# Routed down products with the weights loaded, and their results scattered from PSUM by VectorE and ScalarE

## The chip, the cores and the metric

The kernel runs on one core of a Trainium2 chip. The metric is the device time of one execution in microseconds. Engines: PE (TensorE) multiplies matrices into PSUM; DVE (VectorE), ACT (ScalarE) and POOL (GpSimd) work on elements; SP's queue issues DMAs. Each engine runs its instructions in the order of its program, and they wait for each other through semaphores.

## The reference

Input x has 128 rows (batch) of 32 positions of 128 channels. A first block adds a quantized linear layer on a layer norm to x. What the change touches is the mixture of experts behind it: each of the 128 rows picks two of eight experts, all its 32 positions go through both, and a shared expert runs over all rows.

```python
w, sel = jax.lax.top_k(rw, TOP_K)
w = w / w.sum(axis=-1, keepdims=True)
...
dense_w = jnp.zeros((B, E), x.dtype).at[jnp.arange(B)[:, None], sel].add(w)

def step(acc, params):
    g, u, d, we = params
    return (acc + we[:, None, None] * _gemma_mlp(x, g, u, d), None)
out, _ = jax.lax.scan(step, jnp.zeros_like(x), (skill_gate, skill_up, skill_down, dense_w.T))
out = out + _gemma_mlp(x, shared_gate, shared_up, shared_down)
```

`_gemma_mlp` is gelu(x gate) * (x up), times down, with an inner width of 512. Its sum goes into a last quantized block with 384 inner channels, whose first step needs the largest magnitude of the whole sum.

## The kernel before

**Numbers.** A product of fp32 precision is made of three fast ones: each operand is split in a high part and the rest (`Hh` and `Hl` for the hidden values, plane 0 and 1 of `WD` for the down weights), and high*high, high*low and low*high are added in PSUM.

**Stages.** First (0 to 64 us in the profile) the layer norm, in twelve steps `n`, with the routing worked out beside it on DVE: `S[:, 42]` and `S[:, 43]` become the slots of each row's two choices, `S[:, 38]` and `S[:, 39]` their weights, `ordI` the row of each slot, `etI` the expert of each tile. Then the quantized layer and the first eight steps of the shared expert (`J0` = 2 blocks of four), up to 96 us. Then the routed tiles.

**Routed tiles.** The (row, expert) pairs are sorted by expert into tiles of `SL` = 8 slots; `NM` = 36 tiles are always run. A slot has 32 positions, so a tile is 256 columns. For tile `i`, POOL's `fetch(i)` copies the eight rows' columns from `XT` to `xg`, with the address of each row in a register that is loaded from `ordI`. SP loads the tile's gate and up weights into `Wr`. PE's `unit(i, u)` makes gate and up products into the PSUM banks `BG[u]` and `BU[u]` for u = 0, 1. ACT's `gelu_of` writes `Gb`, DVE's `hidden_of` multiplies with `BU[u]` into `HbS`, ACT's `high_of` makes `Hh`, DVE's `low_of` makes `Hl`. PE's `down(i)` stands after the units of tile `i+1`. The hidden values are loaded as weights and the down weights stream past (256 columns with `Hh`, 128 with `Hl`), at an address in `WD` from a register (`expert_of`). The result has the positions on the partitions. DVE's `sum_y` adds its two halves into `Yb`, and SP's `store_y` writes it to DRAM.

**Rest of the shared expert.** Steps `n` = 8 to 33: PE makes `shared_up(n)` and `shared_down(n-2)`, ACT and DVE the same operations as above on 512 columns. The low part is made by POOL for m < 4 and 16 to 29, else by DVE (`on_pool`). POOL gathers each row's two results from DRAM into `G0` and `G1` by an indirect DMA; ACT scales one, DVE adds the other (`WEIGHS`), PE transposes four blocks of 128 (`TURNS`), and the result is added into `C`. `LARGEST` says at which step the largest magnitude of a block is taken.

**The first turn of a maximum.** At the end of the layer norm DVE reduces eight columns to one (`d_col`), PE transposes it (`turn_max`), DVE reduces again (`top`), and PE spreads the value. PE runs products without use (`busy`) in between. The scale of the quantized layer hangs on this.

Of the kernel before, what the change touches and what calls it, by code (L numbers as in the profile page):

```python
# [14 lines left out]
X = mybir.AxisListType.X  # L15
ADD, SUB, MUL = ALU.add, ALU.subtract, ALU.mult
# [7 lines left out]
XR = 4  # L24
RM = 12582912.0
J0 = 2
EARLY = J0 + 3
# [14 lines left out]
def program(nc, x, cond, Wb, bb, As, Bs, fw, gamma, beta, sg, su, sd, hg, hu, hd, wg, wu, wd, out):  # L42
    ctx = ExitStack()
    with ctx:
# [14 lines left out]
        def sem(name):  # L59
# [6 lines left out]
        X1 = at("X1", [128, T, 128], F32)  # L66
        identF = at("identF", [128, 128], F32)
# [11 lines left out]
        C = at("C", [128, T, 128], F32)  # L79
# [7 lines left out]
        Yb = at("Yb", [128, 4, 2, 128], F32)  # L87
        off[0] = RQ + 24576
        tern = at("tern", [128, 128], BF16)
        SHh = [at(f"SHh{m}", [128, 512], F32R) for m in range(2)]  # L90
# [5 lines left out]
        C_i = at("C_i", [128, 4096], I16)  # L96
# [21 lines left out]
        ioi = at("ioi", [128, NSLOT], I32)  # L118
        bcI = at("bcI", [128, 1], I32)
# [21 lines left out]
        G0 = at("G0", [128, T, 128], F32, R1)  # L141
        G1 = at("G1", [128, T, 128], F32, R1 + 16384)
# [10 lines left out]
        assert RH == R1 + 106496  # L153

        wscr = nc.dram_tensor("wscr", (E * 128, 2048), F32, kind="Internal").ap()
        yscr = nc.dram_tensor("yscr", (SL * NT, 4096), F32, kind="Internal").ap()
# [9 lines left out]
        s_fill = sem("s_fill")  # L166
        s_yw = [sem(f"s_yw{i}") for i in range(4)]
        s_yz = [sem(f"s_yz{i}") for i in range(NT - NM)]
        s_got = [sem(f"s_got{i}") for i in range(4)]
        s_ob = sem("s_ob")  # L170
# [9 lines left out]
        d_rt, d_w2, d_hot, d_absw, d_place, d_parts, d_tern, d_ord, d_et, d_slot = (  # L180
            sem(n) for n in ("d_rt", "d_w2", "d_hot", "d_absw", "d_place", "d_parts", "d_tern", "d_ord", "d_et", "d_slot"))
# [8 lines left out]
        a_wdh, k_wdl = sem("a_wdh"), sem("k_wdl")  # L190
# [4 lines left out]
        k_xg, p_eg, p_eu, a_eg, d_eh, a_ehh, d_ehl, p_ed, d_ey = (  # L195
            sem(n) for n in ("k_xg", "p_eg", "p_eu", "a_eg", "d_eh", "a_ehh", "d_ehl", "p_ed", "d_ey"))
        d_bits, d_k, a_k0, p_kt, a_kc, p_wf, a_wf, d_wf, d_mxc = (
# [30 lines left out]
        def on_pool(m):  # L228
            return m < 4 or 16 <= m <= 29
# [8 lines left out]
        def flat(A, j):  # L238
            return A[:, 4 * j:4 * j + 4, :].rearrange("p t c -> p (t c)")
# [68 lines left out]
        def _(e):  # L308
# [127 lines left out]
            def shared_up(n):  # L436
# [4 lines left out]
                if n >= 2:  # L441
                    w.wait_ge(a_sg, n - 1)
# [1178 lines left out]
```

## Time and profile before

| | us |
|---|---|
| median of 3 runs | 443.53 |
| lowest, highest | 442.97, 444.92 |
| profiled execution | 443.94 |
| its span | 441.9 |
| PE busy | 381.9 (86%) |
| DVE busy | 324.9 (74%) |
| ACT busy | 267.2 (60%) |
| POOL busy | 247.3 (56%) |
| PE's share of the chain that ended last | 64% |

The page splits the span in 40 slices and gives the busy share of each engine in tenths; PE has a 9 in nearly all slices from 110 to 320 us, which are the routed tiles and the shared blocks behind them. Busy shares are means over stages that have different limits, so stretches have to be read one by one. A queue's own instructions (register work, waits) don't count as busy; a view by line names them as POOLq, DVEq or ACTq.

### The profile page before, as it was taken

Reading aid. Unit: us, or ns where it says so; the run is one execution under the profiler, and the core shown is the slowest. Engines: PE = TensorE matmul, PEld = TensorE weight load, DVE = VectorE, ACT = ScalarE, POOL = GpSimd, SP = SyncE. Lnnn points to the kernel's source line nnn. Section 1 sums busy time; section 2 is a strip of 40 time slices with the busy share of each in tenths; the row PEclk is TensorE's granted clock in tenths of the full one; section 3 lists DMA queues with packets and bytes.
Section 4 is the critical chain, followed back from the end, with each engine's and each line's share of the span. In section 5 each row is a group of like instructions: output and inputs, shape, how many; then the busy total and the mean of one; then the engine's idle time right before and its main releaser. Section 6 shows DMA issues by size and latency. Waiting matters only on the chain.

```text
span 441.9 us, 8331 instructions
## 1 busy us (share of the span) xinstructions
PE 381.9 (86%) x2497; PEld 333.0 (75%) x2497; DVE 324.9 (74%) x562; ACT 267.2 (60%) x397; POOL 247.3 (56%) x429
## 2 busy tenths in 40 slices
PE   5888987987999999999999999999999985002997
PEld 4566765667999999999999999877767753001797
DVE  3585647845688877776776776644976989989894
ACT  3556578853545544544544544677647789999660
POOL 1465744856677765665665500744528357895252
PEclk9996999998999999999999999999999999555899
DMA  8799852065677777677677631640000000000022
GB/s 265 281 317 346 306 169 85 1 216 197 233 247 259 248 252 275 233 253 269 229 257 269 229 114 40 227 155 0 0 1 0 0 2 0 1 0 0 1 95 97
DMA packets 30440, 68.14 MB, mean 154 GB/s; under 512 B 3487, under 2 KB 18850, under 8 KB 25762
## 3 DMA queue, kind: packets, MB, share of 16 engines
q1 hardware_dynamic: 27770, 63.19, 41.1%
q0 software_dynamic: 1152, 4.19, 2.7%
q8 instruction: 22, 0.36, 0.3%
q10 hardware_dynamic: 1472, 0.20, 0.3%
q14 instruction: 24, 0.20, 0.1%
HBM read 51.98 MB, written 15.60 MB: 153 GB/s over the span
## 4 chain that ended last, share of the span: by engine, by line
PE 64%; DVE 13%; ACT 8%; POOL 6%; issue 5%; DMA 3%; POOLq 0%; SPq 0%; DVEq 0%; ACTq 0%
PE ps L315 61%; DVE S L671 6%; PE ps L312 3%; DVE O_i L668 1%; ACT xnT L1146 1%; POOL Hl L1367 1%; DMA wscr<-wst 1%; DMA Wr<-wscr 1%; DVE G L662 1%; ACT ps L1146 1%; ACT U L1146 1%; DMA S<-in_cond_dram 1%; DVE S L662 1%; POOL t_i L1364 1%; POOL WD L1367 1%
## 5 line engine op out<-in xcount | busy, mean ns | idle before, releaser
L1424 POOL CAST xg<-XT 128x64 fp32r x288 | 102.3, 404 | 57.8 <-PE ps L315 48.7
L1146 ACT ACTIVATE Gb<-ps 128x512 f32<-128x512 f32 x104 | 62.2, 598 | 92.2 <-PE ps L315 92.0
L315 PE MATMUL ps<-xg,Wr 128*128 128x256 f32 x864 | 112.5, 287 | 3.6 <-issue 2.7
L662 DVE TENSOR_TENSOR HbS<-Gb,ps 128x512 f32<-128x512 f32 x104 | 71.3, 687 | 57.9 <-PE ps L315 56.0
L315 PEld LDWEIGHTS ps<-xg,Wr 128*128 128x128 f32 x864 | 106.9, 193 | 4.2 <-issue 2.9
L1146 ACT ACTIVATE Hh<-HbS 128x512 fp32r<-128x512 f32 x104 | 65.1, 627 | 12.8 <-DVE HbS L662 12.5
L315 PE MATMUL ps<-WD,Hh 128*128 x288 | 68.6, 328 | 0.0
L662 DVE TENSOR_TENSOR Hl<-HbS,Hh 128x512 fp32r<-128x512 f32 x86 | 63.7, 758 | 1.3
L315 PE MATMUL ps<-WD,Hl 128*128 x288 | 64.1, 223 | 0.0
L315 PEld LDWEIGHTS ps<-WD,Hl 128*128 128x128 f32 x288 | 55.2, 192 | 0.0
L315 PEld LDWEIGHTS ps<-WD,Hh 128*128 128x128 f32 x288 | 54.5, 189 | 0.0
L315 PE MATMUL ps<-XT,SHh 128*128 128x512 f32 x144 | 50.9, 405 | 0.0
L1146 ACT ACTIVATE ps<-G,S 128x1024 int32<-128x1024 f32 (+1 forms) x29 | 35.6, 1249 | 6.7 <-DVE O_i L668 6.2
L1367 POOL TENSOR_TENSOR Hl<-HbS,Hh 128x512 fp32r<-128x512 f32 x18 | 23.2, 1291 | 18.1 <-ACT Hh L1146 18.1
L315 PEld LDWEIGHTS ps<-XT,SHh 128*128 128x128 f32 x144 | 27.0, 188 | 5.1
L671 DVE TENSOR_REDUCE S<-G 128x1 f32<-128x1024 f32 (+1 forms) x25 | 28.0, 1165 | 0.6 <-ACT G L1146 0.5
L671 DVE TENSOR_REDUCE Yb<-ps 128x128 f32<-128x256 f32 x72 | 26.7, 410 | 0.6 <-PE ps L315 0.6
L1367 POOL TENSOR_TENSOR wst<-stg,wst 128x512 fp32r<-128x512 f32 x16 | 20.5, 1303 | 9.0 <-ACT wst L1146 9.0
L315 PE MATMUL ps<-XT,SHl 128*128 128x512 f32 x64 | 25.0, 390 | 0.0
L1452 POOL DMA_INDIRECT G<-yscr,sidx x8 | 8.2, 1020 | 28.3 <-issue 28.3
L315 PE MATMUL ps<-Hh,SD 128*128 128x512 f32 x64 | 21.2, 412 | 2.1 <-DVE Hl L662 1.4
L1364 POOL TENSOR_SCALAR G<-O_i 128x1536 f32<-128x1536 int16 (+2 forms) x12 | 12.6, 1047 | 18.0 <-DVE O_i L668 17.9
(191 smaller groups left out, 693.3 us busy)
## 6 DMA issues: line engine op xcount, KB each, us to landing
Wr<-wscr SPq DMA_DIRECT2D x36, 1024.0 KB, 5.0
wscr<-wst SPq DMA_DIRECT2D x16, 512.0 KB, 4.8
yscr<-Yb SPq DMA_DIRECT2D x36, 128.0 KB, 2.7
stg<-n_L_cond_skill_gate_dram SPq DMA_DIRECT2D x8, 256.0 KB, 6.4
stg<-in_L_cond_skill_up_dram SPq DMA_DIRECT2D x8, 256.0 KB, 6.4
wdr<-n_L_cond_skill_down_dram SPq DMA_DIRECT2D x8, 256.0 KB, 4.1
out_dram<-X SPq DMA_DIRECT2D x7, 256.0 KB, 2.0
X<-in_x_dram SPq DMA_DIRECT2D x3, 512.0 KB, 6.8
```

Of the source, the lines that this page charges most:

```text
L312: return e.transpose(o_, i_, identF[:, :])
L315: return e.matmul(o_, l, r, start=start, stop=stop, skip_group_check=True)
L662: return e.tensor_tensor(o_, a, b, op)
L668: return e.scalar_tensor_tensor(out=o_, in0=a, scalar=s, in1=b, op0=op0, op1=op1)
L671: return e.tensor_reduce(o_, i_, X, op, apply_absolute_value=absv)
L1146: return e.activation(o_, i_, func, **kw)
L1364: return e.tensor_scalar(o_, a, s1, s2, op0, op1)
L1367: return e.tensor_tensor(o_, a, hi.bitcast(F32), SUB)
L1424: last = e.tensor_copy(xg[:, i % XR, :, T * s:T * s + T].rearrange("p a t -> p a t"), XT[:, :, :, bass.ds(regs[s], 1)].rearrange("p a t o ...
L1452: e.indirect_dma_start(out=D[:, 8 * p:8 * p + 8, :].rearrange("p t c -> p (t c)"), out_offset=None, in_=yscr.rearrange("n (q c) -> (n q) c ...
```

## The change

The down product of a tile is turned round: the tile's down weights are loaded as PE's weights and the hidden values stream past in 256 columns, so the result has the channels on its partitions and the positions in its columns, as the shared expert's has. PE takes the weights from a fixed place: POOL copies the tile's 1024 columns out of `WD` into one of two buffers `WT` (`down_weights`), which lie where X1 begins. X1 is therefore written to DRAM (`xscr`) before and read back after the last routed tile.

The result stays on the chip. `DD` holds, for each choice, 128 channels by 32 positions by 136 columns, of which 128 are rows. For each slot an operation reads 32 columns of PSUM, multiplies with the slot's weight (`Wt`) and writes them into its row's column of each position, at an address from a register that is loaded from `colI`. Tiles of even number are scattered by DVE, odd ones by ACT. Two new tables are made beside the layer norm: `colI`, the column of each slot, and `Wt`, its weight on all partitions, both by sums over the partitions on PE.

Behind the routed tiles POOL adds the two choices (`PAIRED`), DVE the shared expert's result; the gather, the scaling, the transposes and `C` are gone. POOL makes all low parts of steps 8 to 29. The core of the diff:

```diff
-                for h in range(2):
-                    Z = BY[b][:, 256 * h:256 * h + 256]
-                    both = Z.rearrange("p (a n) -> p a n", a=2)
-                    for q in range(4):
-                        w.wait_ge(d_ehl, 2 * i + 1 + q // 2)
-                        mm(both, Hh[:, 2 * b + q // 2, half(q, h)], WD[:, :, bass.ds(expert[i] + 128 * q, 128)], q == 0, False)
-                        last = mm(Z[:, 0:128], Hl[:, 2 * b + q // 2, half(q, h)], WD[:, 0, bass.ds(expert[i] + 128 * q, 128)], False, q == 3)
+                w.wait_ge(k_wt, i + 1)
+                Z = BY[b][:, 0:256]
+                for q in range(4):
+                    w.wait_ge(a_ehh, 2 * i + 1 + q // 2)
+                    xh, xl = (A[:, 2 * b + q // 2, 256 * (q % 2):256 * (q % 2) + 256] for A in (Hh, Hl))
+                    wh, wl = (WT[:, i % 2, a, 128 * q:128 * q + 128] for a in range(2))
+                    mm(Z, wh, xh, q == 0, False)
+                    mm(Z, wl, xh, False, False)
+                    w.wait_ge(d_ehl, 2 * i + 1 + q // 2)
+                    last = mm(Z, wh, xl, False, q == 3)
...
-            def sum_y(i):
+            def scatter(i):
+
+                w.wait_ge(d_tab, 8)
+                at_ = nc.values_load_multi_w_load_instructions(
+                    colI[0:1, SL * i:SL * i + SL], engines=(mybir.EngineType.DVE,), skip_runtime_bounds_check_because=WHY)[1]
                 w.wait_ge(p_ed, i + 1)
...
+                for s in range(SL):
+                    last = ts(spot(at_[s]), BY[pair(i)][:, T * s:T * s + T], Wt[:, SL * i + s:SL * i + s + 1], None, MUL)
                 last.then_inc(d_ey, 1)
...
+                        if u == 0 and i >= 2 and i % 2:
+                            scatter(i - 2)
...
+            def down_weights(i):
+
+                at_ = nc.values_load_multi_w_load_instructions(
+                    etI[0:1, 0, i:i + 1], engines=(mybir.EngineType.Pool,), skip_runtime_bounds_check_because=WHY)[1][0]
...
+                e.tensor_copy(WT[:, i % 2, :, :], WD[:, :, bass.ds(at_, 512)]).then_inc(k_wt, 1)
...
-            busy(12, bank[2], WbTh[:, :], xTh[:, 0, :])
+            w.wait_ge(d_tab, 6)
+            mm(bank[4][0:1, 0:NSLOT], ones[:, 0:1], tmpP[:, :], True, False)
+            mm(bank[4][0:1, 0:NSLOT], ones[:, 0:1], tmpQ[:, :], False, True).then_inc(p_tab, 1)
+            mm(bank[3][:, 0:NSLOT], ones[:, :], Pm[:, :], True, False)
+            mm(bank[3][:, 0:NSLOT], ones[:, :], iof[:, :], False, True).then_inc(p_tab, 1)
+            busy(7, bank[2], WbTh[:, :], xTh[:, 0, :])
...
+                if m in PAIRED:
+                    j = PAIRED[m]
+                    w.wait_ge(*spread_of(NM - 2))
+                    w.wait_ge(*spread_of(NM - 1))
+                    e.tensor_tensor(choice(0, j), choice(0, j), choice(1, j), ADD).then_inc(k_dd, 1)
```

How the instructions stand is shown at three places. PE, one down product of the routed stage, before (WD down weights, Hh and Hl hidden values, ISA a register instruction; the pair of products comes eight times, the first four times with ISA ahead):

```order
L315 ISA [waits d_ehl,d_ey]
L315 MATMUL ps<-WD,Hh 128x256
L315 MATMUL ps<-WD,Hl 128x128
L315 ISA
L315 MATMUL ps<-WD,Hh 128x256
L315 MATMUL ps<-WD,Hl 128x128
L315 ISA [waits d_ehl]
```

and now, all of it (WT the copied down weights):

```order
L341 MATMUL ps<-Hh,WT 128x256 [waits a_ehh,k_wt,d_ey]
L341 MATMUL ps<-Hh,WT 128x256
L341 MATMUL ps<-Hl,WT 128x256 [waits d_ehl]
L341 MATMUL ps<-Hh,WT 128x256 x2
L341 MATMUL ps<-Hl,WT 128x256
L341 MATMUL ps<-Hh,WT 128x256 [waits a_ehh]
L341 MATMUL ps<-Hh,WT 128x256
L341 MATMUL ps<-Hl,WT 128x256 [waits d_ehl]
L341 MATMUL ps<-Hh,WT 128x256 x2
L341 MATMUL ps<-Hl,WT 128x256
```

Sixteen products with register addresses became twelve without, and they wait for POOL's copy (k_wt).

DVE, one tile of the same stage before (Yb the summed down result):

```order
L671 TENSOR_REDUCE Yb<-ps 128x128 [waits p_ed,s_yw1]
L671 TENSOR_REDUCE Yb<-ps 128x128
L662 TENSOR_TENSOR HbS<-Gb,ps 128x512 [waits a_eg,d_ehl,p_eu] x2
L662 TENSOR_TENSOR Hl<-HbS,Hh 128x512 [waits a_ehh] x2
L662 TENSOR_TENSOR WQ<-WQ,S 128x1152 [waits d_bits]
```

and now the end of an odd tile and the start of an even one (colI the table of columns, DD the scattered result; the last two rows come six times more, then HbS follows):

```order
L672 TENSOR_TENSOR HbS<-Gb,ps 128x512 [waits a_eg,d_ehl,p_eu] x2
L672 TENSOR_TENSOR Hl<-HbS,Hh 128x512 [waits a_ehh] x2
L675 TENSOR_SCALAR S_54<-S_54 128x36 [waits d_bits]
L962 TENSOR_LOAD colI
L675 ISA [waits p_ed]
L675 ISA x2
L675 TENSOR_SCALAR DD<-ps,Wt 128x32
L675 ISA x3
L675 TENSOR_SCALAR DD<-ps,Wt 128x32
```

Two reductions per tile became, every second tile, one load of registers, 24 register instructions and eight small operations, and they stand ahead of the tile's HbS.

ACT, two tiles of the same stage before (Gb the Gelus, Hh the high parts):

```order
L1146 ACTIVATE Gb<-ps 128x512 [waits p_eg] x2
L1146 ACTIVATE Hh<-HbS 128x512 [waits d_eh,p_ed]
L1146 ACTIVATE Hh<-HbS 128x512 [waits d_eh]
L1146 ACTIVATE Gb<-ps 128x512 [waits p_eg] x2
L1146 ACTIVATE Hh<-HbS 128x512 [waits d_eh,p_ed]
```

and now the end of an even tile and the start of an odd one, again with six more of the last two rows, then the second Gb:

```order
L1169 ACTIVATE Hh<-HbS 128x512 [waits d_eh,p_ed]
L1169 ACTIVATE Hh<-HbS 128x512 [waits d_eh]
L1169 ACTIVATE Gb<-ps 128x512 [waits p_eg]
L1274 TENSOR_LOAD colI
L1169 ISA [waits p_ed]
L1169 ISA x2
L1169 ACTIVATE DD<-ps,Wt 128x32
L1169 ISA x3
L1169 ACTIVATE DD<-ps,Wt 128x32
```

The same instructions as DVE's now stand between the two Gelus of every second tile.

## Rows read from the trace of the kernel before

**Rows 1.** Stretches, us: busy (instructions) of PE, PEld, DVE, ACT, POOL; clock; DMA; GB/s.

```profile
110.00:268.00 158.00, 158.00 (x1342) 158.00 (x1340) 120.48 (x207) 79.31 (x135) 90.94 (x249) 1.00 0.68 237
268.00:328.00 60.00, 58.62 (x283) 46.80 (x282) 40.77 (x65) 38.01 (x68) 26.23 (x22) 1.00 0.22 76
```

**Rows 2.** Timeline, a tile: start, length, engine, line, operation, out<-in, idle before.

```profile
188.18 3.08 PE L315 MATMUL ps<-xg,Wr 128*128 128x256 f32 x24
189.15 0.60 ACT L1146 ACTIVATE Gb<-ps 128x512 f32<-128x512 f32 x1 [1.21 <-PE ps L315]
189.88 0.69 DVE L662 TENSOR_TENSOR HbS<-Gb,ps 128x512 f32<-128x512 f32 x1 [0.48 <-PE ps L315]
...
191.07 0.62 ACT L1146 ACTIVATE Hh<-HbS 128x512 fp32r<-128x512 f32 x1
191.10 0.28 PE L315 MATMUL ps<-WD,Hh 128*128 x1
...
191.91 1.53 DVE L662 TENSOR_TENSOR Hl<-HbS,Hh 128x512 fp32r<-128x512 f32 x2
...
192.90 3.08 PE L315 MATMUL ps<-xg,Wr 128*128 128x256 f32 x24
193.37 0.74 DVE L671 TENSOR_REDUCE Yb<-ps 128x128 f32<-128x256 f32 x2
```

**Rows 3.** Timeline of POOL, three fetches that follow each other.

```profile
111.06 2.95 POOL L1424 CAST xg<-XT 128x64 fp32r x8 [0.93 <-PE ps L315]
114.39 1.97 POOL L1424 CAST xg<-XT 128x64 fp32r x8 [0.38 <-PE ps L315]
117.72 2.01 POOL L1424 CAST xg<-XT 128x64 fp32r x8 [1.36 <-issue]
```

**Rows 4.** Lines L1416, L916, L1238, their queue instructions: ns shortest/median/longest.

```profile
L1416 POOLq FUSED_REGOPS  x288: 147/147/185, 90.3 to 246.6; - x144
L1416 POOLq TENSOR_LOAD <-ordI x36: 561/565/1718, 89.5 to 244.4; - x36
...
L916 DVEq FUSED_REGOPS  x1: 222/222/222, 93.7 to 93.7; - x1
...
L1238 ACTq FUSED_REGOPS  x1: 167/167/167, 95.5 to 95.5; - x1
```

**Rows 5.** Groups by shape: busy us, mean ns of one, idle time before.

```profile
L665 DVE TENSOR_SCALAR ST<-ps 128x4 f32<-128x4 f32 x8 | 1.2, 154 | 3.9 <-PE ps L315 3.8
L668 DVE SCALAR_TENSOR_TENSOR Pm<-iof,S,tmpP 128x312 f32<-128x312 f32 x1 | 0.6, 610 | 0.0
L665 DVE TENSOR_SCALAR tmpP<-iof,S 128x312 f32<-128x312 f32 x1 | 0.4, 366 | 0.0
...
L315 PE MATMUL ps<-hs,BT 128*128 128x512 f32 x16 | 8.3, 603 | 0.0
...
L1424 POOL CAST xg<-XT 128x64 fp32r x288 | 102.3, 404 | 57.8 <-PE ps L315 48.7 <-issue 9.1
L1367 POOL TENSOR_TENSOR Hl<-HbS,Hh 128x512 fp32r<-128x512 f32 x18 | 23.2, 1291 | 18.1 <-ACT Hh L1146 18.1
L1364 POOL TENSOR_SCALAR U_i<-U,S 128x1024 int16<-128x1024 f32 x12 | 13.3, 1127 | 0.6 <-DVE S L1112 0.3 <-POOL t_i L1364 0.2
```

**Rows 6.** Timeline, the last maximum of the layer norm and its first turn.

```profile
62.45 0.69 DVE L671 TENSOR_REDUCE S<-xnT 128x1 f32<-128x512 f32 x1 [0.79 <-ACT xnT L1146]
...
63.39 0.27 PE L312 MATMUL ps<-identF,S 128*1 128x128 f32 x1 [0.29 <-DVE S L671]
...
64.34 1.88 PE L315 MATMUL ps<-xTh,WbTh 128*128 128x512 f32 x7
```

**Rows 7.** Chain that ended last: start, us, what.

```profile
277.71 2.08 PE ps L315 x9
...
292.90 0.45 PE ps L312 x4
...
297.98 0.45 PE ps L312 x4
```

More of the change, by code:

```diff
@@ L24 @@
 XR = 4
+DW = 136
 RM = 12582912.0
 J0 = 2
-EARLY = J0 + 3
 class Waits:
@@ L165, in program @@
         s_wz = [sem(f"s_wz{i}") for i in range(NT - NM)]
[L166 to L170, printed above, removed]
+        s_xs = [sem(f"s_xs{i}") for i in range(2)]
+        s_xr, s_ob = sem("s_xr"), sem("s_ob")
         k_const, d_const = sem("k_const"), sem("d_const")
@@ L217, in program @@
         NG, NR, HK = 2 * E, 2 * E + 3, 4 * J0
-        IOTA, PART, TRI0, IDENT, TRI, CTR, HALVES, MEAN = 3, 4, 5, 6, 7, 8, 9, 10
+        IOTA, PART, TRI0, IDENT, TRI, CTR, HALVES, MEAN, PLACES = 3, 4, 5, 6, 7, 8, 9, 10, 11
         SPLITS = (0, 2, 2, 3, 3, 2, 2, 2, 0, 3, 0, 0)
-        WEIGHS = {16: 5, 18: 6, 20: 7, 22: 0, 24: 1, 25: 2, 27: 3, 28: 4}
-        TURNS = {n + 2: j for n, j in WEIGHS.items()}
-        LARGEST = {25: (0,), 26: (5,), 27: (1,), 28: (2,), 30: (3,), 32: (6, 4), 33: (7,)}
-        WEIGHED = list(WEIGHS.values())
-        ENDED = [0, 5, 1, 2, 6, 3, 4, 7]
+        ENDED = [2, 0, 3, 1, 4, 5, 6, 7]
+        PAIRED = {9: 2, 11: 0, 13: 3, 15: 1, 17: 4, 19: 5, 21: 6, 23: 7}
+        ADDED = list(PAIRED.values())
+        LARGEST = {14: 2, 16: 0, 18: 3, 20: 1, 22: 4, 26: 5, 30: 6, 33: 7}
+        WHY = "made from the slots' rows alone"
         def on_pool(m):
-            return m < 4 or 16 <= m <= 29
+            return m < 4 or HK <= m <= 29
         def low_at(m):
@@ L827, in _ @@
                     w.wait_ge(d_rt, n_)
-                    for p in range(4):
-                        ts(sidx[:, 2 * p:2 * p + 2], S[:, 42:44], 4.0, float(p), MUL, ADD).then_inc(d_slot, 1)
                 if n == 5:
@@ L984, in _ @@
                         low_of(i, u)
-                    w.wait_ge(s_yw[i % 4], 16 * (i // 4))
-                    sum_y(i)
-                for r in range(NT - NM):
-                    w.wait_ge(s_yz[r], 16)
+                    if i % 2 == 0:
+                        scatter(i)
             w.passed = passed
@@ L1246, in high_of, with scatter @@
                 do(Hh[:, 2 * pair(i) + u, :], HbS[:, u, :]).then_inc(a_ehh, 1)
+            def scatter(i):
+                w.wait_ge(d_tab, 8)
+                at_ = nc.values_load_multi_w_load_instructions(
+                    colI[0:1, SL * i:SL * i + SL], engines=(mybir.EngineType.Activation,), skip_runtime_bounds_check_because=WHY)[1]
+                w.wait_ge(p_ed, i + 1)
+                for s in range(SL):
+                    last = do(spot(at_[s]), BY[pair(i)][:, T * s:T * s + T], ACT.Identity, scale=Wt[:, SL * i + s:SL * i + s + 1])
+                last.then_inc(a_ey, 1)
             for i in range(NM + 1):
@@ L1264, in _ @@
                     shared_high(HK)
+            scatter(NM - 1)
             passed = dict(w.passed)
@@ L1274, in _ @@
                         high_of(i, u)
-                w.wait_ge(d_ey, NT)
-                for r in range(NT - NM):
-                    w.wait_ge(s_yz[r], 16)
+                    if i % 2:
+                        scatter(i)
             w.passed = passed
```

235 lines of the change are left out of this document (114 added, 121 removed).

## The prediction, made before the changed kernel ran

> **What bounds the kernel now.** I read the table of stretches first. From 110 to 268 us, the stage of the routed tiles, PE is busy for all 158.00 us, at full granted clock, while DVE is busy for 120.48, ACT for 79.31 and POOL for 90.94 [rows 1]. So in this stage PE sets the pace, and the other engines wait for it. The timeline of one tile shows the pace: the gate and up products of one tile start at 188.18 and those of the next at 192.90, so a tile takes 4.72 us. Its 24 gate and up products fill 188.18 to 191.10, 0.122 us each; its 16 down products fill the other 1.80 us, 0.1125 each, although half of them have only 128 columns [rows 2]. In the same rows one sees the chain that runs beside PE: the first Gelu on ACT 0.60 us, the product Gb*up on DVE 0.69, the high part on ACT 0.62, two low parts on DVE 1.53 together, two sums of the down result 0.74. DVE has 1.38 + 1.53 + 0.74 = 3.65 us of work per tile and ACT 1.20 + 1.25 = 2.45, so both have over a microsecond to spare. The next stage, 268 to 328, is also PE's (58.62 of 60.00 busy) [rows 1].
>
> **What it means to address by a register.** This change lives on it, so I price it before anything else. POOL already does it in the kernel before: one fetch is 33 instructions that are not waits (a TENSOR_LOAD of eight numbers, 16 register instructions, then eight times one register instruction and a copy). Where POOL isn't held by others, fetches start at 111.06, 114.39 and 117.72, which is 3.33 us apart, although the eight copies take only 1.97 to 2.95 us of that [rows 3]. The difference is the register work: at POOL's queue a TENSOR_LOAD takes 565 ns and each of the eight larger register instructions 147 ns [rows 4]. So a slot costs (3.33 - 0.565) / 8 = 0.35 us in the queue of POOL, far more than its arithmetic.
>
> The changed kernel's scatter of one tile has again 33 such instructions: one TENSOR_LOAD, and eight times three register instructions and one small operation. The small operation itself is short: a DVE operation of 128x4 out of PSUM took 154 ns [rows 5], eight would be 1.2 us. The queue is what costs. The same larger register instruction, seen once each, took 222 ns on DVE and 167 ns on ACT against 147 on POOL [rows 4]. Scaled by that, a slot is 0.35 x 222/147 = 0.52 us on DVE and 0.39 on ACT; unscaled it is 0.35 on both. I take the middle of each, 0.43 on DVE and 0.37 on ACT, since the two scaled values rest on one instance each; the ends stay in the range. A scatter is then 8 x 0.43 = 3.44 us on DVE and 8 x 0.37 = 2.96 on ACT, with a TENSOR_LOAD of 0.57 ahead of each. These eight groups stand behind the wait for the down product, so they can't be done early by the program's order.
>
> The Trainium skill (Advanced Engine Details and Errata, Clock Domains) has VectorE's sequencer at 0.96 GHz where the others run at 1.2, a factor of 1.25; by that a DVE slot would be 0.44 us. The rows agree in direction (222 against 147) and go further.
>
> **Part 1, the down products.** Now 12 products of 256 columns per tile in place of 16 (the change's section shows the order). At 0.122 us each that is 1.46 us in place of 1.80, and PE's tile falls from 4.72 to 36 x 0.122 = 4.39 us: -0.33 us per tile, if PE stays what sets the pace. PE also loses its own register work, which was hidden already since PE was never idle [rows 1].
>
> **Part 2, the scatters, which I expect to set the pace.** Even tiles go to DVE, ahead of the two products Gb*up of the tile two later; odd ones to ACT, between its two Gelus. Both engines run their queues in order, so each scatter holds up everything behind it, and the chain passes from one to the other. Over two tiles, from one DVE scatter to the next: the scatter 3.44; both Gb*up of the even tile 2 x 0.69 = 1.38; hand-over to ACT 0.13 (a Gelu ends at 189.75, DVE starts at 189.88 [rows 2]; I use this for all four); the high part and the Gelu of the odd tile are only passed on to ACT's data path, then its TENSOR_LOAD 0.57; the ACT scatter 2.96; the second Gelu 0.60; hand-over 0.13; Gb*up 0.69; 0.13; high part 0.63; 0.13; the low part is only passed on, then DVE's TENSOR_LOAD 0.57, and the next scatter follows. Sum 11.36 us for two tiles. PE needs 2 x 4.39 = 8.78 for them and the kernel before takes 9.44. So this closed chain is the longest, and the tile takes 5.68 us. PE then waits at the up products, because the bank of the last one is freed by the Gb*up that stands behind the scatter. There are 17 such pairs: 17 x (11.36 - 9.44) = **+33 us**. With 0.35 for every slot the pair is 10.5 us and the term +18; with 0.52 and 0.39, and 0.3 more for DVE's TENSOR_LOAD, 12.5 us and +52.
>
> What goes with the scatters: the sums (0.74 us of DVE per tile [rows 2]), the stores of the tiles, the gather; none of them held PE, so they give nothing back. SP loses the stores and gets eight writes of X1 before the first tile and eight reads after the last, both far from any wait that ends late.
>
> **Part 3, POOL.** Behind each fetch stands a copy of the tile's down weights, 128x1024. Its queue costs 0.57 + 0.35 = 0.92 us; with the fetch 4.25 us per tile, under 5.68, and the copy itself (a POOL operation of that size took 1.13 us [rows 5]) runs beside the next register work. The weights of a tile are copied two tiles ahead. I cost this at nothing; if its cover is gone it is a rival below.
>
> **Part 4, the tables, before 64 us.** DVE gets six operations of 128x312 in the last steps of the layer norm. One of them took 0.61 and a simpler one 0.37 us [rows 5]. Two (0.98) stand straight ahead of the last product xnT, one (0.37) between the last maximum and the overall one; the rest falls into DVE's idle time. So the last maximum, at 62.45 in [rows 6], ends near 64.1 and the last table operation near 64.5. PE waits for that operation, then makes four products of 312 columns in full fp32 and seven fillers, and only then turns the maximum. A full fp32 product of 512 columns is two of the 16 instructions that took 8.3 us [rows 5], so 1.04 us, and 0.63 for 312 columns: 2.5 us; seven fillers took 1.88 [rows 6]. The turn comes at 64.5 + 2.5 + 1.9 = 68.9 in place of 63.39: +5.5. All that follows hangs on this scale. Two more DVE operations in the quantization add about 0.3. **+5.8 us**, 4 to 7.
>
> **Part 5, the rest of the shared blocks, 268 to 328.** Eight groups of four transposes leave, 0.45 us each: -3.6. In three places PE waited for POOL's low part behind ACT's extra copies (the chain has 5.08 us from the transposes at 292.90 to those at 297.98, for two steps of 2.08 and four transposes of 0.45, 4.6 us; so again twice after that [rows 7]): -1.4. But POOL now makes all the low parts (1.29 us each [rows 5]) and eight adds of the same size between them. A step is 2.08 us, and two low parts and one add take 3.9 of 4.16; the low part behind an add comes about 0.5 us late, and PE has nearly no slack for it: +4. At the start the last ACT scatter stands ahead of a Gelu: +1.5. Sum +0.5, from -4 to +3.
>
> **The sum.** The profiled execution took 443.94 us (span 441.9). 443.9 + 33 + 5.8 + 0.5 = 483.2. The median of the runs is 0.4 lower: **483 us**.
>
> **Rivals.**
> Faster: the register work runs beside the data paths and the scatters cost only their small operations. Then PE sets the pace, a pair takes 8.78, 17 x -0.66 = -11; with parts 4 and 5 it is 439 us. For it: PE's register work was hidden entirely. The Trainium skill (Advanced Engine Details and Errata, Sequencer and Instruction Queues) says too that other engine instructions can be queued while a control instruction is executed; the trace agrees only in that copies of 1.97 and of 2.95 us give the same 3.33. Against it: POOL's fetches are 3.33 us apart with 1.97 of copies [rows 3]. It decides at the price of a slot: the pair without slots is 4.96 us, so the change as a whole loses nothing once a pair is at most 9.44 - 6.3/17 = 9.07, which is 0.26 us per slot. Chance 0.14.
> Each engine alone: the slots cost what I say, but the scatters overlap in time rather than follow each other. DVE's queue is 2 x (1.38 + 1.53) + 3.44 = 9.2 us per pair: 443.9 - 4 + 6.3 = 446. Against it: the second Gb*up needs the Gelu behind ACT's scatter. Chance 0.09.
> POOL: copy, register work and fetch add up instead of overlapping, 3.33 + 0.92 + 1.13 = 5.4 us per tile, and copies on POOL stretch: their mean is 404 ns [rows 5], while undisturbed they follow each other by 0.25 [rows 3]. With 0.9 more, 6.3 us: 470 to 500 us. The Trainium skill (SBUF — State Buffer) says that a VectorE instruction with two SBUF inputs contends with a GpSimd one that reads SBUF, which DVE's low parts are; the 404 ns agree with it. Chance 0.08.
>
> **How the numbers follow.** The forecast, 462 to 507 by its bounds (443.9 + 18 + 4 - 4, and + 52 + 7 + 3), has 0.69, POOL's case 0.08, the single engines 0.09, the faster one 0.14. A measurement of this kernel can tell about 0.5%, 2.2 us, from no change. Faster 0.14; within it 0.05, from the 446 case; slower 0.81. The range goes from 446 to 505 and leaves out the faster case and the top of the forecast.
>
> **What would show it.** In the profile after: PE busy for some 75 to 80% of the routed stage, waiting for DVE's Gb*up at the up products; two tiles in 11.4 us; DVE's and ACT's small operations at 0.35 to 0.52 us from one to the next although each takes under 0.25; POOL with idle time; the first turn of a maximum near 69 us. I am wrong if the small operations follow each other at under 0.26 us, if PE stays without a gap, or if DVE's and ACT's scatters lie in the same time.

## The result, and the profile after

The changed kernel took 476.4 us (median of 4 runs, 475.0 to 479.1) beside 444.2 us for the kernel before (4 runs): 1.074 times the time before, with a 95% interval of 1.067 to 1.080. The prediction was 483 us, slower. The profiled execution took 479.12 us (span 477.3), the slowest of the four; before it was 443.94 (span 441.9).

First the table of stretches of the changed kernel, with the columns of [rows 1]:

```profile
66.00:73.00 7.00, 7.00 (x17) 3.81 (x16) 0.00 (x0) 0.24 (x2) 0.00 (x0) 0.56 0.34 138
116.00:300.00 184.00, 158.18 (x1216) 154.94 (x1216) 132.52 (x278) 111.57 (x265) 126.91 (x293) 0.95 0.53 187
```

In the routed stage PE is busy for 86% of the time where it was busy for all of it [rows 1], and its granted clock is 0.95. (The prediction's sign was 75 to 80%; products at the lower clock take longer and count as busy all the while.) The new first row is a stretch in which PE works at 0.56 of its clock and DVE and ACT do nothing; I come back to it. Who waits for whom is in the table of waits (us in total, times, longest):

```profile
ACT Hh L1169 <- DVE HbS L672: 70.4, 39, 4.2
POOL WT L1467 <- PE ps L341: 46.3, 26, 5.0
DVE HbS L672 <- ACT Gb L1169: 37.4, 21, 3.6
...
PE ps L341 <- DVE HbS L672: 26.8, 17, 2.5
```

ACT waits for DVE, DVE waits for ACT, and PE waits 17 times for DVE's `HbS`: once in each pair of tiles but the first, and once behind the last, in the shared blocks. POOL waits for PE. That is a closed chain of two engines with PE behind it. One pair, in the timeline:

```profile
184.78 2.85 DVE L675 TENSOR_SCALAR DD<-ps,Wt 128x32 f32 x8
...
187.52 1.27 DVE L672 TENSOR_TENSOR HbS<-Gb,ps 128x512 f32<-128x512 f32 x2
188.25 2.42 PE L341 MATMUL ps<-xg,Wr 128*128 128x256 f32 x18 [0.42 <-DVE HbS L672]
188.29 1.17 ACT L1169 ACTIVATE Hh<-HbS 128x512 fp32r<-128x512 f32 x2 [2.70 <-DVE HbS L672]
...
189.85 2.49 ACT L1169 ACTIVATE DD<-ps,Wt 128x32 f32 x8
...
192.92 0.69 DVE L672 TENSOR_TENSOR HbS<-Gb,ps 128x512 f32<-128x512 f32 x1 [1.97 <-ACT Gb L1169]
...
195.35 3.08 DVE L675 TENSOR_SCALAR DD<-ps,Wt 128x32 f32 x8 [0.31 <-issue]
```

It reads as the prediction's chain: DVE's scatter, the product Gb*up behind it, ACT's scatter between its two Gelus, the second Gelu, and DVE's product that waited 1.97 us for it. The chain of work that ended last goes through two of DVE's products in each pair, one behind DVE's scatter and one behind ACT's. Of those behind ACT's, the first, two in the middle and the last are

```profile
116.02 0.70 DVE HbS L672
...
182.13 0.70 DVE HbS L672
...
192.92 0.69 DVE HbS L672
...
302.75 0.70 DVE HbS L672
```

so 17 pairs take 302.75 - 116.02 = 186.7 us, **10.98 us a pair** (predicted 11.36; 9.44 before).

A mean hides that the pairs are of two kinds, long ones and short ones; that is taken up further on. The rest of the difference is found by landmarks that both programs have: the last square of the layer norm, the first turn of a maximum [rows 6], the first product of the first tile, the first product of the remaining shared blocks, the overall maximum, the end. Such a table takes out the start of the program, up to the last square, which took between 55.8 and 60.4 us in thirteen profiles whatever the kernel, and which hides differences of a few us in single executions.

| stretch, us | before | after | difference | predicted |
|---|---|---|---|---|
| start to last square | 56.07 | 56.20 | +0.1 | 0 |
| to the first turn | 7.32 | 16.63 | +9.3 | +5.5 |
| to the first tile | 32.53 | 35.67 | +3.1 | +0.3 |
| the routed tiles | 172.50 | 194.34 | +21.8 | +33 |
| remaining shared blocks, to the maximum | 60.58 | 62.13 | +1.6 | +0.5 |
| to the end | 112.90 | 112.33 | -0.6 | 0 |
| sum (span) | 441.9 | 477.3 | +35.4 | +39.3 |

The landmarks of after, from its timeline:

```profile
72.83 0.28 PE L338 MATMUL ps<-identF,S 128*1 128x128 f32 x1
...
108.50 7.48 PE L341 MATMUL ps<-xg,Wr 128*128 128x256 f32 x48 [2.02 <-DMA Wr<-wscr]
...
302.84 0.40 PE L341 MATMUL ps<-XT,SHh 128*128 128x512 f32 x1
```

### The profile page after: what moved, and what is told of

Its sections match the earlier page's. It is cut to its first block, busy times and chain, and to the rows that moved or that the text cites. A ratio compares the mean times of both kernels' runs of the same rounds, so it can differ in the third digit from the quotient of the medians.

```text
span 477.3 us, 8947 instructions
## 1 busy us (share of the span) xinstructions
PE 385.0 (81%) x2324; PEld 328.4 (69%) x2324; DVE 329.4 (69%) x622; ACT 295.7 (62%) x527; POOL 297.7 (62%) x474
## 4 chain that ended last, share of the span: by engine, by line
DVE 26%; PE 25%; ACT 19%; issue 12%; POOL 9%; DMA 4%; DVEq 3%; ACTq 2%; POOLq 0%; SPq 0%
PE ps L341 23%; ACT Hh L1169 6%; DVE DD L675 5%; DVE HbS L672 5%; ACT DD L1169 5%; DVE S L681 4%; DVE Hl L672 4%; DVEq L675 3%; ACT Gb L1169 3%; POOL Hl L1393 2%; ACTq L1169 2%; PE ps L338 2%; DMA wbr<-in_L_cond_W_base_dram 1%; DVE O_i L678 1%; DMA Wr<-wscr 1%
## 5 line engine op out<-in xcount | busy, mean ns | idle before, releaser
L341 PE MATMUL ps<-xg,Wr 128*128 128x256 f32 x864 | 122.0, 298 | 27.8 <-DVE HbS L672 25.8
L341 PEld LDWEIGHTS ps<-xg,Wr 128*128 128x128 f32 x864 | 115.2, 205 | 31.5 <-DVE HbS L672 29.1
L1467 POOL CAST WT<-WD 128x1024 fp32r x36 | 38.2, 1062 | 48.0 <-PE ps L341 46.3
L341 PE MATMUL ps<-Hh,WT 128*128 128x256 f32 x288 | 55.3, 290 | 0.0
L675 DVE TENSOR_SCALAR DD<-ps,Wt 128x32 f32 x144 | 38.4, 277 | 18.6 <-issue 5.5
L1393 POOL TENSOR_TENSOR Hl<-HbS,Hh 128x512 fp32r<-128x512 f32 x26 | 34.4, 1324 | 24.8 <-ACT Hh L1169 24.8
L341 PEld LDWEIGHTS ps<-Hh,WT 128*128 128x128 f32 x288 | 47.0, 200 | 0.1
L1169 ACT ACTIVATE DD<-ps,Wt 128x32 f32 x144 | 44.9, 321 | 1.9 <-issue 1.2
L341 PE MATMUL ps<-Hl,WT 128*128 128x256 f32 x144 | 41.5, 288 | 0.0
L1169 ACT ACTIVATE ps<-G,S 128x1024 int32<-128x1024 f32 (+1 forms) x29 | 35.6, 1249 | 6.0 <-DVE O_i L678 5.4
L341 PEld LDWEIGHTS ps<-Hl,WT 128*128 128x128 f32 x144 | 28.6, 198 | 0.0
L341 PE MATMUL ps<-XT,SHl 128*128 128x512 f32 x64 | 26.2, 409 | 0.0
```

The source lines that it names most:

```text
L341: return e.matmul(o_, l, r, start=start, stop=stop, skip_group_check=True)
L675: return e.tensor_scalar(o_, a, s1, s2, op0, op1)
L1169: return e.activation(o_, i_, func, **kw)
L1393: return e.tensor_tensor(o_, a, hi.bitcast(F32), SUB)
L1467: e.tensor_copy(WT[:, i % 2, :, :], WD[:, :, bass.ds(at_, 512)]).then_inc(k_wt, 1)
```

## The experiments

Two theories for the 21.8 us: the **closed chain** (two scatters that follow each other through DVE and ACT) against its rivals (POOL's queue, each engine's own queue, register work that costs nothing). And for the 12.4 us ahead of the first tile: the tables, in PE's part or in DVE's. All experiments start from the changed kernel, the last four with two repairs in it. They ran on two chips: known addresses, ACT's scatter at the end of the tile, more work for POOL and both parts of the tables moved on one, all others on the other. Ratios are to the kernel before on the same chip, which took 442.1 us on the first and 443.1 to 443.4 on the second.

### Addresses known in advance

```diff
-                at_ = nc.values_load_multi_w_load_instructions(
-                    colI[0:1, SL * i:SL * i + SL], ...)[1]
+                at_ = [(8 * (i // 2) + s) % 128 for s in range(SL)]
...
-                    last = ts(spot(at_[s]), BY[pair(i)]...
+                    last = ts(DD[:, at_[s]:at_[s] + DW * (T - 1) + 1:DW], BY[pair(i)]...
```

(ACT's likewise.) 

> The changed kernel with scatters that write to columns known in advance: the same eight small operations of 128x32 on DVE or ACT for each tile, at the same places of the queues, but no TENSOR_LOAD and no register instruction. It leaves out the placement by token; all else is computed. Theory that the register work in the queue sets the price: the small operations follow each other at 0.15 to 0.2 us, the scatter falls from 2.8 us on DVE and 2.5 on ACT to 1.2 to 1.6, the loads of 0.6 go, the closed chain of two tiles falls from the measured 10.98 us to about 8.2, below PE's 8.78, and PE sets the pace: 17 x -2.2 = -37, so 439 us. Rival, that the operation itself costs what its row says (277 ns on DVE, 321 on ACT): two tiles take about 10.1 and the time is 461. Rival, that POOL sets the pace: 470 or more.

Measured: 435.6 us (434.5 to 436.9), 0.984 of before (0.978 to 0.991). One scatter of each engine in its timeline:

```profile
197.59 1.38 DVE L675 TENSOR_SCALAR DD<-ps,Wt 128x32 f32<-128x32 f32 x8
...
201.26 1.57 ACT L1168 ACTIVATE DD<-ps,Wt 128x32 f32<-128x32 f32 x8
```

Eight operations take 1.38 and 1.57 us, 0.17 and 0.20 each, although a single one still shows 269 and 344 ns: they overlap. PE's groups of 24 products start at 191.21, 195.53 and 199.85, so a tile takes 4.32 us, PE's 36 products at 0.12. The routed stage takes 155.26 us. The stage of the changed kernel took 191.5 to 194.3 us in its profiles, so its scatters cost it 36 to 39 us by their register addressing. The rest of the change gives 17 us there against before (172.5 - 155.3): 36 tiles of 0.40 us less are 14.4 of them, the others lie in a hole of the kernel before that comes up below. The theory that the register work sets the price holds; both rivals (461 and 470 or more) fell, and the time is 3 us under the 439 that I expected.

### ACT's scatter at the end of the tile

```diff
                         gelu_of(u, 2 * i + u + 1)
-                        if u == 0 and i >= 2 and i % 2:
-                            scatter(i - 2)
...
                         high_of(i, u)
+                    if i >= 2 and i % 2:
+                        scatter(i - 2)
```

> The changed kernel with one call moved on ACT: the scatter of an odd tile stands behind the two high parts of the tile, at its end, no longer between its two Gelus. No instruction is added or removed. Theory of the closed chain: the second Gb*up no longer waits for ACT's scatter, DVE's and ACT's scatters lie in the same time, and DVE's own queue, 2 x (1.38 + 1.38) + 2.85 + 0.57 = 8.9 us, or PE with 8.78, sets the pace in place of 10.98 for two tiles: 17 x -1.9 to -2.2, so 439 to 444 us. Rival, that one engine's own queue sets the pace already (each engine alone, or POOL): nothing changes, 476.

Measured: 450.9 us (446.6 to 451.7), 1.020 (1.014 to 1.026). Not an instruction less, and the routed stage takes 165.4 us, 26 to 29 less than the changed kernel's 191.5 to 194.3. The timeline shows both scatters in the same time:

```profile
190.06 2.60 ACT L1169 ACTIVATE DD<-ps,Wt 128x32 f32 x8 [0.26 <-issue]
...
190.87 3.08 DVE L675 TENSOR_SCALAR DD<-ps,Wt 128x32 f32 x8 [0.19 <-issue]
...
193.84 1.28 DVE L672 TENSOR_TENSOR HbS<-Gb,ps 128x512 f32<-128x512 f32 x2
```

and the products behind DVE's scatter start at 184.69, 193.84 and 202.99: 9.15 us a pair, DVE's own queue (expected 8.9; the two low parts of a tile took 1.81 and 1.39 us in this pair where I had 1.38). The closed chain stands, and "the queue of one engine sets the pace" falls for the changed kernel: it became nearly true only here, where DVE still waits 0.16 us for ACT's high parts in each tile. The time misses my 439 to 444. The pair above was 0.25 us longer than my sum, and others are longer still: from 118.25 to 267.34 the 16 pairs take 8.8 to 10.4 us, 9.32 in the mean, which is 7 us in all. And I had started from 476.4, while the changed kernel took 480.4 when it ran again (below, on the other chip).

### ACT's scatter behind both Gelus, ahead of the high parts

```diff
-                        if u == 0 and i >= 2 and i % 2:
+                        if u == 1 and i >= 2 and i % 2:
```

> The changed kernel with ACT's scatter behind both Gelus of the odd tile but still ahead of its two high parts. Nothing is added or removed. Theory of the closed chain: the high parts now wait for the scatter, the low parts for them, and DVE's next scatter stands behind these: from one DVE scatter to the next 2.9 + 0.69, up and gate of the odd tile on PE 1.5, Gelu 0.6, ACT's load and scatter 0.5 + 2.4, two high parts 1.2, low part 0.8, about 10.5 us in place of 10.98, so 470 to 478 us. Rival, that only the second Gelu matters and everything behind it has slack: as with the scatter at the tile's end, 447 to 452.

Measured: 483.1 us (480.9 to 486.7), 1.087. The rival (447 to 452) fell, and the time is also above my 470 to 478. The chain was longer than my sum of 10.5: its pairs took 11.00 to 12.29 us, 11.36 in the mean from 133.55 to 303.97. Even the short ones are 0.5 above the sum, which I can't place. In the long ones PE's half clock is one of the reasons, since here a link of the chain runs through PE. In the pair from 191.01 to 202.50, 11.49 us, it was slow:

```profile
191.75 3.45 PE L341 MATMUL ps<-xg,Wr 128*128 128x256 f32 x18 [2.13 <-DVE HbS L672]
```

18 products in 3.45 us; in the changed kernel's pair above they took 2.42. So it is not enough to take the scatter from between the Gelus; it has to stand behind everything that DVE waits for.

### More work for POOL, and the changed kernel again

```diff
+                if i:
+                    w.wait_ge(k_wt, i)
+                for s in range(2 if i >= 2 else 0):
+                    e.tensor_copy(scr[:, 2, s, :], WDf[:, bass.ds(at_, 32)])
                 e.tensor_copy(WT[:, i % 2, :, :], WD[:, :, bass.ds(at_, 512)]).then_inc(k_wt, 1)
```

> The changed kernel with more work on POOL: ahead of each copy of down weights from the third tile on two more register-addressed copies of 128x32, about 0.35 us each in its queue, 0.7 us for each tile. Theory: POOL waits for PE for over a microsecond in each tile and has room for it: no change, 476 us, within 1.5 us. Rival, that POOL's queue is part of what sets the pace: 34 x 0.7 = 24 us more, 500.

> The changed kernel itself once more, as the measure for the runs beside it. The start of the program (the loads of the weights up to the last square of the layer norm) has taken between 56 and 60 us in the profiles so far, whatever the kernel; so single profiles are compared stretch by stretch from that square on, and times on the same chip. By the first runs 476.4 us beside 444.2; the kernel with more work on POOL took 479.1 beside 442.1. Theory that POOL has room: this run too comes to 477 to 480 beside it, and the routed stage takes the same 191.5 us. Rival, that POOL's extra work did cost: 473 to 475 here.

Measured: 479.1 us (477.0 to 480.8) with the extra copies, 480.4 (476.9 to 482.7) without. The groups of the first show that the work was done and where its time came from:

```profile
L1472 POOL COPY scr<-WD 128x32 f32 x68 | 14.1, 237 | 33.5 <-PE ps L343 27.5 <-issue 5.7
```

POOL still waited 27.5 us for PE ahead of them, and the routed stage took 191.5 us (193.0 without). POOL is no part of the chain. (The time is above my 476 by 3 us, and so is that of the changed kernel itself.) The two ran on different chips, so the stage and the ratios (1.085 and 1.080, intervals 1.078 to 1.092 and 1.071 to 1.088) say more than the times. 480.4 us is also the measure for the runs on the second chip, 4 us more than the first time; the first chip has none of its own.

### The tables moved

PE's part alone: the four products stand behind the first shared blocks, where PE waits for `Wr`, and the twelve fillers are back (DVE's two operations that read their results go with them).

```diff
             w.wait_ge(a_zg, 8)
-            w.wait_ge(d_tab, 6)
-            mm(bank[4][0:1, 0:NSLOT], ones[:, 0:1], tmpP[:, :], True, False)
...
-            busy(7, bank[2], WbTh[:, :], xTh[:, 0, :])
+            busy(12, bank[2], WbTh[:, :], xTh[:, 0, :])
             turn_max(0, bank[6], S[:, 180:181])
```

> The changed kernel with only PE's part of the tables moved: the four products stand behind the first shared blocks and the twelve fillers ahead of the first turn again, while DVE's six table operations stay where the change put them. From the last square to the first turn: 7.3 us before, 15.2 to 16.6 with the change, 8.0 to 8.4 with both parts moved. Theory: DVE's operations ahead of the last product xnT cost 2.3 us and the one ahead of the overall maximum 0.4, PE's wait, its products at half its clock and its fillers the rest; so 10.0 us from the last square to the turn, and 475 us beside the 480.4 of the changed kernel. Rival, that DVE's operations are most of it: 13 us or more, and 478.

With DVE's part too: `tmpQ` behind the last product `xnT`, `Pm` and `iof` behind the scale.

> The changed kernel with its tables moved: PE makes the four table products after the last product of the first shared blocks, ahead of the first tile, where it waits for Wr anyway; PE has its twelve fillers ahead of the first turn of a maximum again, and DVE makes the last three table operations behind the last product xnT and behind the scale, not ahead of them. The scatters are as they were. The changed kernel's first turn stood at 72.83 us, that of the kernel before at 63.39. My theory: those 9.4 us come back, less 0.3 to 1 for the operations in their new places, and of the 3.1 us that the stretch from the turn to the first tile got longer some 1 to 2, because PE's granted clock was lower there; from 476.4 to between 465 and 468 us, with the turn at 63.5 to 64.5. By the prediction's own size for this part it would be 5.8 us: 470.6. Rival: the late start is absorbed further on, since the first tile waits for its weights: 473 to 476.

Measured: 470.4 us (468.2 to 471.6) for PE's part alone, beside 480.4 for the changed kernel on that chip, and 472.0 us (469.4 to 472.3) for both on the other chip. Both times miss what I expected, 475 and 465 to 468. The two can't be told apart by their times, but can by the stretch from the last square to the turn, which came out at 9.78 us where I expected 10.0:

| us | before | change (6 profiles) | PE's part moved | both moved (5 profiles) |
|---|---|---|---|---|
| last square to first turn | 7.32 | 15.2 to 16.6 | 9.78 | 8.0 to 8.4 |
| turn to first tile | 32.53 | 33.7 to 35.7 | 33.58 | 33.4 to 34.4 |

So PE's part costs 5.4 to 6.8 us and DVE's operations 1.4 to 1.8. How PE's part came to that is in the changed kernel's timeline:

```profile
61.11 0.97 DVE L678 SCALAR_TENSOR_TENSOR tmpQ<-iof,S,tmpQ 128x312 f32<-128x312 f32 x1
62.01 1.38 DVE L675 TENSOR_SCALAR Pm<-iof,S 128x312 f32<-128x312 f32 x1
...
64.77 0.69 DVE L681 TENSOR_REDUCE S<-xnT 128x1 f32<-128x512 f32 x1 [0.79 <-ACT xnT L1169]
...
65.95 1.20 PE L341 MATMUL ps<-tmpP,ones 128*1 128x312 f32 x2 [5.46 <-DVE iof L675]
...
69.91 3.08 PE L341 MATMUL ps<-xTh,WbTh 128*128 128x512 f32 x7
```

PE waited 5.46 us for the last table operation, and then ran at the lower clock: its four products filled 65.95 to 69.9 (3.9 us; I had 2.5) and seven fillers took 3.08 us where seven of the same products took 1.88 before [rows 6]. The kernel before kept PE at work here; the change took five of the twelve fillers away and put a wait in their place.

### Both repairs, and what could be had beyond

> Both repairs together: ACT's scatter at the end of the odd tile and the tables behind the first shared blocks. If the two terms are independent, the stretch from the last square to the first turn takes 8.4 us (15.4 without it), the 36 tiles 9.15 us for two, and the time is 450.9 - 7 = 444 us, 441 to 446; that is the time of the kernel before. Rival, that the start is then held by the weights of the first tile: 448 to 451.

> The kernel with both repairs once more, as the measure for the run beside it and against the kernel before: 441 us beside 443 by the first time (0.995 of it). Theory: the two terms, 26 to 30 us from the scatters' chain and 7 to 8 from the tables, are all that the change lost; what is left is 2 us less than before, from PE's tile that fell from 4.72 to 4.58. So 0.993 to 0.997 of the kernel before.

Measured: 441.2 us (10 runs, 438.0 to 443.5), 0.995 of before (0.991 to 0.999), and 440.3 (12 runs), 0.996 (0.992 to 1.000). The terms are independent: against the 480.4 us of the changed kernel one alone gave 29.5, the other 8.4 (both on the other chip), and both together 39.2. Together they are what the change lost. Stretches: 8.0 to the turn, 165.7 for the routed tiles in both.

In the next one DVE also makes the low parts that stand behind POOL's adds:

```diff
-            return m < 4 or HK <= m <= 29
+            return m < 4 or HK <= m <= 29 and m - 1 not in PAIRED
```

> The kernel with both repairs (ACT's scatter at the tile's end, tables late), and in the remaining shared blocks DVE makes the eight low parts that stand behind an add of POOL's; POOL keeps the adds and the other low parts. In the profile with both repairs PE waited 0.6 us for POOL's low part in every second step, and the stretch from the first of the remaining shared blocks to the overall maximum took 61.0 us, before the change 60.6. Theory that POOL's adds cost there what the taken away turns had given: the eight waits go, the stretch falls by 3 to 5 us to 56 to 58, and the time by as much: 437 us beside 441. Rival, that DVE, which also has the sums and maxima, is late instead: 441 or more.

Measured: 438.4 us (12 runs, 437.2 to 439.4), 0.992 of before (0.988 to 0.995). The remaining shared blocks took 59.0 us in place of 61.1; I had expected 56 to 58. Low parts that stand behind POOL's adds did delay PE there, by 2 us and not by 3 to 5. This is the fastest version that computes everything.

The last try shared each tile's eight results, on top of both repairs (three by DVE, five by ACT a tile later):

```diff
-                for s in range(SL):
+                for s in range(3):
                     last = ts(spot(at_[s]), ...)
...
-                for s in range(SL):
-                    last = do(spot(at_[s]), ...)
+                for s in range(3, SL):
+                    last = do(spot(at_[s - 3]), ...)
```

> As the one before, but each tile's eight results are shared: three go by DVE at the end of the next tile, five by ACT at the end of the tile after that, behind DVE's (both read one PSUM bank, so they do it one after the other). DVE's queue for two tiles is 2 x (1.38 + 1.38 + 3 x 0.36 + 0.4) = 8.5 us, ACT's 2 x (1.2 + 1.25 + 5 x 0.31 + 0.45) = 8.9, PE's 8.64; two loads per tile in place of one are its price. Theory that the longest queue sets the pace: 8.9 to 9.2 for two tiles, 17 x -0.1 = -2 at best against 9.15, 438 to 446 us. Rival, that the wait of ACT's part for DVE's closes a chain again: 455 or more.

Measured: 457.8 us (455.3 to 459.8), 1.032 (1.026 to 1.038): a miss. The chain of work that ended last shows what closed:

```profile
190.52 0.70 DVE HbS L673
...
191.30 1.17 ACT Hh L1168 x2
...
195.24 0.47 ACT Gb L1168
...
195.83 0.70 DVE HbS L673
```

DVE's product, ACT's two high parts, ACT's load and scatter, its next Gelu, DVE's next product: 5.0 to 5.3 us for each tile. The scatter stood behind the high parts and ahead of the next Gelu. With the scatter in every second tile this ring would be passed once in a pair and the other tile catch up; with one in every tile it sets the pace. That is my reading, and no run takes the ring apart. The rival's number came true, 455 or more, but not its cause: no wait of ACT for DVE's part stands in the chain. And the loads got dearer, not cheaper:

```profile
L1273 ACTq TENSOR_LOAD <-colI x36: 1114/1122/1141, 109.7 to 285.4; - x36
```

## Why the prediction was right

**What bounds.** Right: PE no longer sets the pace; it waits at the up products for `HbS`, in 16 of the 17 pairs.

**The price of a slot.** Right in kind and close in size. The chain of the changed kernel has DVE's operations at 184.96, 185.36 and 185.76, so 0.40 us a slot (I took 0.43); ACT's follow each other by 0.33 (I took 0.37, and 0.35 was the low end of my sign):

```profile
184.96 0.21 DVE DD L675
...
185.36 0.21 DVE DD L675
...
190.39 0.16 ACT DD L1169
...
190.71 0.16 ACT DD L1169
```

The instructions of one scatter of each, in the windows 184.1 to 187.5 and 189.4 to 192.2 (ns shortest/median/longest, first and last start):

```profile
L675 DVEq FUSED_REGOPS  x16: 52/118/183, 184.2 to 187.3; - x16
L675 DVEq SEQ_ASSERT  x8: 23/23/23, 184.4 to 187.2; - x8
L675 DVE TENSOR_SCALAR DD<-ps,Wt x8: 272/278/283, 184.8 to 187.4; 128x32 f32 x8
...
L1169 ACTq FUSED_REGOPS  x16: 42/94/147, 189.4 to 191.9; - x16
L1169 ACTq SEQ_ASSERT  x8: 18/18/18, 189.6 to 191.9; - x8
L1169 ACT ACTIVATE DD<-ps,Wt x8: 317/322/325, 189.8 to 192.0; 128x32 f32 x8
```

The larger register instruction took 183 ns on DVE, not the 222 of its single instance before, and 147 on ACT, not 167 [rows 4]: as much as POOL's. That is a factor of 1.24 for DVE; the Trainium skill (Advanced Engine Details and Errata, Clock Domains) gives 1.25 for DVE's sequencer, and this trace agrees. The three queue instructions of a slot add up to 183 + 23 + 52 = 258 ns on DVE and 147 + 18 + 42 = 207 on ACT; the rest of the 0.40 and 0.33 us lies between them. The small operation, 0.28 and 0.32 us long, runs beside the larger instruction of the next slot, which the trace has some 0.02 us behind its start. So what I had assumed, that the queue's work hides the operation, held. With addresses known in advance the same slots take 0.17 and 0.20: the register work made them 0.23 and 0.13 us longer.

**The closed chain.** Right, and shown by the two moves of ACT's scatter. The term was too large, 33 for 21.8. The pair from 182.13 to 192.92 can be set beside my sum link by link:

| link, us | predicted | measured |
|---|---|---|
| HbS, high part, low part passed on, DVE's load, to its first register instruction | 2.15 | 2.05 |
| DVE's scatter, to the next HbS | 3.44 | 3.34 |
| two HbS, high part and Gelu passed on, ACT's load, to its first register instruction | 2.08 | 1.90 |
| ACT's scatter, to the second Gelu | 2.96 | 2.78 |
| Gelu, to HbS | 0.73 | 0.72 |
| pair | 11.36 | 10.79 |

Every link is there, each a little shorter, and nothing was counted that isn't. The loads of addresses in particular are in the chain as I had them. DVE's starts right behind the start of its low part at 183.52 and runs beside it, but it takes the queue for 597 ns, and the first register instruction stands at 184.18. Of what the Trainium skill states (Advanced Engine Details and Errata, Sequencer and Instruction Queues: other engine instructions can be read and queued while a control instruction is executed) no run here shows a case, since each small operation needs the register that the control instructions ahead of it write; what the trace shows is an operation handed over earlier that goes on beside them.

The shortest pairs took these 10.79 us, the mean 10.98, 26.2 us more than before for 17 pairs. The excess isn't PE's clock. The chain goes from one of DVE's products to the next but one in steps of half a pair:

```profile
170.97 0.69 DVE HbS L672
...
176.72 0.69 DVE HbS L672
...
182.13 0.70 DVE HbS L672
...
187.52 0.69 DVE HbS L672
```

24 of the 34 half pairs took 5.39 to 5.43 us and ten took 5.68 to 5.76. The half from 176.72, in which PE made 18 products in 3.76 us at half its clock (last section), took 5.41. The half before took 5.75, and it has a gap in DVE's own slots that nothing in the profile ends:

```profile
173.40 0.28 DVE L675 TENSOR_SCALAR DD<-ps,Wt 128x32 f32 x1 [0.29 <-issue]
...
174.15 2.67 DVE L675 TENSOR_SCALAR DD<-ps,Wt 128x32 f32 x7 [0.47 <-issue]
```

In the second profile of the changed kernel the same ten halves are the long ones, so the gaps belong to places of the program and not to PE's clock. What makes them stays open; they are 3.3 us of the stage.

And 4.4 us of gain lay outside the pairs (172.5 - 17 x 9.44 = 12.0 before, 194.3 - 186.7 = 7.6 after): the kernel before had a hole at its second tile that the change closed, and behind it products at the lower clock,

```profile
101.70 4.60 PE L315 MATMUL ps<-xg,Wr 128*128 128x256 f32 x24 [2.68 <-issue]
```

while the changed kernel makes the 48 products of its first two tiles in one run. The prediction read only the steady part of the stage. What opened the hole before, the profile doesn't name. So my 32.6 (17 x 1.92) became 21.8: 9.7 less by the links, 3.3 more by the gaps, 4.4 less outside the pairs.

**The down products.** I had 0.33 us a tile; PE's tile is 4.32 us where nothing else holds it, 0.40 less than 4.72.

**POOL.** Right: no cost.

**The tables.** The mechanism right, the size wrong: 8 to 9.3 us for 5.5. The step that failed is "0.63 for 312 columns: 2.5 us; seven fillers took 1.88": both durations came from rows at the full clock, while the same step made PE wait for 5.46 us first, and the runs show 3.9 and 3.08 us in their place. The two DVE operations ahead of `xnT` took 2.35 us for 0.98 while POOL worked beside them. So the turn came at 72.83 and not at 68.9: 1.4 us by the products, 1.2 by the fillers, the rest by DVE's operations. In the stretch behind, the turn to the first tile, I had +0.3 for +3.1. By six profiles with the change, it took 33.7 to 33.8 us where the granted clock was 1.00, 34.9 at 0.95 and 35.6 to 35.7 at 0.90, as in this one: so up to 1.9 us are the clock. The other 1.2 stand at full clock too; PE's wait for `Wr` ahead of the first tile, 1.9 to 2.1 us in all six for 0.97 before, is most of them.

**The shared blocks.** +1.6 for +0.5 in this profile, within its bounds, but this is the least that was seen: the stretch took 62.1 to 64.5 us in the six profiles that keep ACT's scatter between or behind the Gelus, up to +3.9, which is above my +3. With the scatter at the end of the tile it took 61.0, and with addresses known in advance 58.5. So the last scatters weigh more there than my 1.5, and the low parts behind the adds, measured alone, less: 2 us for my 4. The other two parts weren't measured.

**The rivals.** The free register work decides at 0.26 us a slot by my sum: the slots are above that, and the run with addresses known in advance, where they cost 0.17 and 0.20, is on the other side, faster than before. Each engine alone and POOL fell.

The bounds of the forecast add up to 506, not to the 507 that stands there; nothing hangs on it.

In all, 39.3 us were predicted for the 35.4 of the profile: a scatter term 11 too large stood against tables and start 7 too small. The size of the total owes something to that.

## What to carry to other kernels

A small operation that is addressed by a register cost 0.40 us on DVE and 0.33 on ACT here, for work that took 0.17 and 0.20 with a constant address; count the slots, then ask which instruction of another engine stands behind them. Where two engines feed each other in turn, put such a block behind the last thing that the other engine waits for: here that alone was worth 26 to 29 us and cost nothing. And don't price work behind a new wait of PE by rows at the full clock alone; ask too whether PE is in the chain there, for in the routed stage it was not.

## What was not expected of the hardware

PE's granted clock fell behind some waits of PE in the middle of a stage that is dense otherwise, and not behind others of the same length. Four pairs of the changed kernel, and a stretch in the first of them:

```profile
177.45 3.76 PE L341 MATMUL ps<-xg,Wr 128*128 128x256 f32 x18 [2.54 <-DVE HbS L672]
...
210.13 2.42 PE L341 MATMUL ps<-xg,Wr 128*128 128x256 f32 x18 [2.19 <-DVE HbS L672]
...
242.80 3.92 PE L341 MATMUL ps<-xg,Wr 128*128 128x256 f32 x18 [2.18 <-DVE HbS L672]
...
264.76 2.42 PE L341 MATMUL ps<-xg,Wr 128*128 128x256 f32 x18 [2.26 <-DVE HbS L672]
...
178.00:180.00 2.00, 2.00 (x12) 2.00 (x11) 1.84 (x3) 1.99 (x7) 0.23 (x1) 0.50 0.02 4
```

Behind the wait of 2.54 us PE ran at 1.2 GHz (0.50) and made 18 products in 3.76 us. Behind one of 2.26 us it kept 2.4 GHz and took 2.42. Behind six of the 16 waits of the stage, 0.40 to 2.54 us long, the 18 products took 3.08 to 3.92 us. Those six waits were 1.90 to 2.54 us long, but behind five others of 1.89 to 2.26 us the products took 2.41 or 2.42. So the length of the wait alone doesn't say it here.

The time of a load of register values does not go by their number: one value took 300 ns (PE) and 292 (POOL), eight took 548 (ACT) and 597 (DVE), but three took 747 (DVE) and five 1122 (ACT), in the kernel with shared results.
